# Attention and product-key experts on one core: heads summed in two groups by TensorE, attention's sums inverted on ScalarE, and new orders on every engine

## The reference, cut to what matters

```
q   = xn @ wq.T                       # 2 halves, 8 heads, 64 wide
sim = q . keys                        # per half and head 32 scores
sx, ix = top_k(sim[0], 16);  sy, iy = top_k(sim[1], 16)
scores, pk = top_k(sx[:, None] + sy[None, :], 16)     # of 256 pairs
h   = gelu(xn . table_down[indices]) * softmax(scores)
out = sum over 8 heads and 16 picks of h * table_up[indices]
```

## Time and profile before

| | us |
|---|---|
| median of 3 runs | 1073.86 (1070.39 to 1075.57) |
| the profiled execution, own time | 1074.99 |
| its span, first to last instruction | 1073.2 |
| VectorE busy | 931.1 |
| TensorE busy (matmuls) | 764.6 |
| ScalarE busy | 704.9 |
| GpSimd busy | 656.5 |
| mean granted clock of TensorE | 0.89 |

### The profile page before, as it was taken

One profiled execution on the slowest core, in us unless ns is written; L12 is line 12 of the kernel. 1 busy time (PEld: TensorE's weight loads), 2 busy tenths in 40 slices (PEclk: granted clock), 3 DMA queues, 4 the chain that ended last, 5 costly groups with the idle time before them and its releaser, 6 DMA issues.

```text
span 1073.2 us, 22148 instructions
## 1 busy us (share of the span) xinstructions
PE 764.6 (71%) x6014; PEld 474.0 (44%) x6014; DVE 931.1 (87%) x4054; ACT 704.9 (66%) x1008; POOL 656.5 (61%) x371
## 2 busy tenths in 40 slices
PE   3672868686777878586777768686767878776374
PEld 2431525354444535354444535354444545353253
DVE  3327289999999999899999989899999989998987
ACT  1352677676867676676867676676867676756461
POOL 2101077694948576694948576694948576674942
PEclk9695979898998989898999989898998989797766
DMA  5312103030212103030212102030212102000000
GB/s 145 51 21 34 17 13 38 1 52 1 39 15 37 16 13 40 0 53 1 38 15 38 16 14 40 0 53 1 39 15 38 16 13 37 1 11 2 5 1 10
DMA packets 51538, 26.51 MB, mean 25 GB/s; under 512 B 5168, under 2 KB 51120, under 8 KB 51312
## 3 DMA queue, kind: packets, MB, share of 16 engines
q1 hardware_dynamic: 51504, 26.11, 15.0%
HBM read 19.93 MB, written 5.24 MB: 23 GB/s over the span
## 4 chain that ended last, share of the span: by engine, by line
DVE 38%; PE 34%; ACT 12%; issue 11%; DMA 1%; SPq 1%; POOL 1%; DVEq 1%; ACTq 0%; POOLq 0%
DVE prob L910 13%; DVE late_scores L777 6%; PE misc L1131 5%; ACT prob L640 4%; PE score L1192 4%; PE score L1081 4%; PE score L1111 3%; PE score L1161 3%; PE score L1204 2%; DVE cand L856 2%; PE misc L1133 2%; DVE cand_left L874 2%; ACT late_scores L544 2%; PE misc L1220 2%; DVE halves L771 2%
## 5 line engine op out<-in xcount | busy, mean ns | idle before, releaser
L449 POOL TENSOR_TENSOR acc<-acc,prob 128x1024 f32<-128x1024 f32 x186 | 441.7, 2375 | 16.6 <-DVE prob L910 0.5
L910 DVE SCALAR_TENSOR_TENSOR prob<-score,cut,prob 128x1024 f32<-128x1024 f32 x256 | 316.7, 1277 | 37.4 <-ACT prob L640 36.0
L640 ACT ACTIVATE prob<-score,neg_lse,unit 128x1024 f32<-128x1024 f32 x256 | 299.4, 1201 | 65.4 <-PE score L1192 51.3
L1192 PE MATMUL score<-sel,pieces_t 128*128 128x512 f16 x512 | 177.3, 447 | 102.3 <-DVE prob L910 97.5
L561 ACT ACTIVATE probs<-score 128x512 f32<-128x512 f32 x192 | 107.6, 599 | 64.7 <-PE score L1113 63.2
L422 POOL TENSOR_TENSOR scale<-bounded,half_neg 128x2 f32<-128x2 f32 x16 | 11.2, 703 | 202.7 <-DVE bounded L821 202.7
L1192 PEld LDWEIGHTS score<-sel,pieces_t 128*128 128x128 f16 x512 | 43.3, 108 | 183.6 <-DVE prob L910 151.6
L544 ACT ACTIVATE late_scores<-score 128x512 bf16<-128x512 f32 x128 | 69.6, 594 | 67.3 <-PE score L1084 62.2
L1111 PE MATMUL score<-q_stack,k_stack 128*128 128x512 bf16 x192 | 76.1, 401 | 45.9 <-DVE prob L910 23.5
L1081 PE MATMUL score<-k_ahead,q_ahead 128*128 128x256 bf16 (+1 forms) x512 | 75.9, 253 | 44.3 <-ACT probs L561 18.8
L449 POOL TENSOR_TENSOR acc<-prob 128x1024 f32<-128x1024 f32 x31 | 73.2, 2361 | 44.2 <-DVE prob L910 44.2
(11 more groups left out here) (119 smaller groups left out, 1549.4 us busy)
## 6 DMA issues: line engine op xcount, KB each, us to landing
q_ahead<-q_scratch SPq DMA_DIRECT2D x96, 64.0 KB
q_stack<-q_scratch SPq DMA_DIRECT2D x96, 64.0 KB
q_scratch<-qk_piece SPq DMA_DIRECT2D x16, 192.0 KB, 2.4
xin<-x SPq DMA_DIRECT2D x16, 128.0 KB, 4.7
xres<-x SPq DMA_DIRECT2D x16, 128.0 KB, 5.1
out<-fin SPq DMA_DIRECT2D x16, 128.0 KB, 5.6
k_ahead<-qk_piece SPq DMA_DIRECT2D x96, 4.0 KB
k_stack<-qk_piece SPq DMA_DIRECT2D x96, 4.0 KB
```

The source lines that it names most:

```text
L449: eng.tensor_tensor(acc[:, j, :], so_far, prob[:, j * FH + h, :], ALU.add).then_inc(acc_added, 1)
L640: eng.activation(prob[:, g, :], score[g % BUFS][:, :], ACT.Exp, bias=neg_lse[:, j, h:h + 1], scale=unit[:, :]).then_inc(prob_made, 1)
L910: eng.scalar_tensor_tensor(prob[:, g, :], score[g % BUFS][:, :], cut[:, j, h:h + 1], prob[:, g, :], ALU.is_ge, ALU.mult).then_inc(prob_mas ...
L1192: ins = eng.matmul(score[g % BUFS][:, cols], pieces_t[:, j, h, :], sel[:, cols], start=True, stop=True)
```

## The change

The heads of a tile are no longer added into one tensor. GpSimd adds heads 1, 2, 3 onto head 0 and 5, 6, 7 onto head 4, in place in `prob` (six additions a tile, `ADDS` = 6), and `acc` is gone. TensorE makes the transposed sum: for each of the eight blocks it multiplies the group's block with the identity twice, and PSUM accumulates. Head 0 and head 4 of a tile may be overwritten a batch later only when TensorE has read them (`acc_tp`). VectorE's additions of the last tile go the same way.

The inverse of attention's sums is Ln and then Exp with scale -1 on ScalarE (`invert_sums`), not a reciprocal on VectorE. `select_pairs` is split into `sum_pairs` (the five additions and the size) and the selection.

The orders change on four engines: on GpSimd make_xhat comes ahead of make_xn; on ScalarE the inversion stands behind the copies of x2 and ahead of all twelve score copies, `best_exp` of tile 0 among these, `activate` behind `log_sum`; on VectorE ln1 and make_y come directly behind the second key selection, ahead of the candidates, and the folding ahead of the second tile's candidates; on TensorE the value matmuls come directly behind attention's scores, then the scores for the maxima with project_y and the second tile's sums among them. The diff, cut to its core:

```diff
+GROUP = 4
+ADDS = FH - FH // GROUP
+def added(j, h):
+    return j * ADDS + h - h // GROUP
...
             def add_head(b, j, h):
                 eng.wait_ge(prob_masked, at(prob_masked, b, j * FH + h + 1))
-                ...
-                eng.tensor_tensor(acc[:, j, :], so_far, prob[:, j * FH + h, :], ALU.add).then_inc(acc_added, 1)
+                if h % GROUP > 1:
+                    eng.wait_ge(acc_added, at(acc_added, b, added(j, h - 1)))
+                group = prob[:, j * FH + h - h % GROUP, :]
+                eng.tensor_tensor(group, group, prob[:, j * FH + h, :], ALU.add).then_inc(acc_added, 1)
...
             def iteration(i, d, f, a, m, p):
-                if a:
-                    make_xn(i + 1)
                 if p:
                     make_xhat(i + 3)
                 if a:
+                    make_xn(i + 1)
                     sim_low_piece(i + 1, 0)
...
+            def invert_sums(b):
+                eng.wait_ge(av_made, every(av_made, b))
+                if later(b):
+                    eng.wait_ge(proj_made, at(proj_made, b, 0))
+                eng.activation(y_t[:, :], misc[0][:, T:2 * T], ACT.Ln).then_inc(y_log, 1)
+                eng.wait_ge(y_log, every(y_log, b))
+                eng.activation(y_t[:, :], y_t[:, :], ACT.Exp, scale=-1.0).then_inc(y_inverse, 1)
...
             def pair_probs(b, j, h):
-                    eng.wait_ge(acc_added, at(acc_added, b - 1, j * (FH - 1) + max(h, 1)))
+                    if h % GROUP:
+                        eng.wait_ge(acc_added, at(acc_added, b - 1, added(j, h)))
+                    else:
+                        eng.wait_ge(acc_tp, at(acc_tp, b - 1, j + 1))
...
                 if f:
                     pieces_back(i, 1)
-                if m:
-                    for u in range(6):
-                        max_scores_back(i + 2, u)
                 if d and f:
                     age_x2(i - 1)
                 if f:
                     copy_x2(i)
+                if a:
+                    invert_sums(i + 1)
                 if m:
-                    for u in range(6, MAX_STEPS):
+                    copy_v(i + 2)
+                    for u in range(9):
                         max_scores_back(i + 2, u)
-                    copy_v(i + 2)
                 if f:
+                    best_exp(i, 0)
+                if m:
+                    for u in range(9, MAX_STEPS):
+                        max_scores_back(i + 2, u)
+                if f:
+                    log_sum(i, 0)
                     activate(i, 0)
                     activate(i, 1)
...
             def make_y(b):
-                if later(b):
-                    eng.wait_ge(proj_made, at(proj_made, b, 0))
                 eng.wait_ge(av_made, every(av_made, b))
-                eng.reciprocal(y_t[:, :], misc[0][:, T:2 * T]).then_inc(y_inverse, 1)
                 eng.wait_ge(y_inverse, every(y_inverse, b))
...
                 if f:
                     select_keys(i, 1)
+                if p:
+                    ln1(i + 3)
+                if a:
+                    make_y(i + 1)
+                if f:
+                    sum_pairs(i, 0)
                     select_pairs(i, 0)
                 if a:
-                    make_y(i + 1)
+                    make_x2(i + 1)
                 if d:
                     gate(i - 1, 1)
-                if a:
-                    make_x2(i + 1)
-                if f:
-                    select_pairs(i, 1)
+                if f:
                     sum_best(i, 0)
-                if p:
-                    ln1(i + 3)
-                if f:
-                    log_sum_exp(i, 0)
                 if m:
                     fold_max(i + 2, 0, 6)
                 if f:
+                    sum_pairs(i, 1)
+                    log_sum_exp(i, 0)
+                    select_pairs(i, 1)
+                if f:
+                    mask(i, 0, 0)
+                    mask(i, 0, 1)
                     sum_best(i, 1)
-                    for h in range(4):
-                        mask(i, 0, h)
+                    mask(i, 0, 2)
+                    mask(i, 0, 3)
                     log_sum_exp(i, 1)
...
                 for c in range(CH):
-                    ins = eng.transpose(score[j][:, c * P:(c + 1) * P], acc[:, j, c * P:(c + 1) * P], ident[:, :])
+                    for h in range(0, FH, GROUP):
+                        ins = eng.matmul(score[j][:, c * P:(c + 1) * P], prob[:, j * FH + h, c * P:(c + 1) * P],
+                                         ident[:, :], start=h == 0, stop=h == FH - GROUP)
...
-                if m:
-                    for u in range(6):
-                        scores_for_max(i + 2, u)
                 if a:
                     weigh_values(i + 1, 0, piece_t_made, i)
                     weigh_values(i + 1, 1, piece_t_made, i)
                 if m:
-                    for u in range(6, MAX_STEPS):
+                    for u in range(4):
+                        scores_for_max(i + 2, u)
+                if a:
+                    project_y(i + 1, piece_t_made, i)
+                if m:
+                    for u in range(4, 8):
                         scores_for_max(i + 2, u)
                 if d:
                     acc_transposes(i - 1, 1)
+                if m:
+                    for u in range(8, MAX_STEPS):
+                        scores_for_max(i + 2, u)
                 if f:
                     hidden_units(i, 0)
-                if a:
-                    project_y(i + 1, piece_t_made, i)
-                if f:
                     hidden_units(i, 1)
                 if a:
                     xn_transpose(i + 1, y_t_made, i + 1)
                 if f:
-                    pair_scores(i, 0, 0, a, m)
+                    for h in range(3):
+                        pair_scores(i, 0, h, a, m)
...
                 if p:
                     project_qkv(i + 3, sim_kept, i + 1)
                 if f:
-                    for h in range(5, FH):
-                        pair_scores(i, 0, h, a, m)
+                    pair_scores(i, 0, 5, a, m)
+                    pair_scores(i, 0, 6, a, m)
+                if p:
+                    eng.wait_ge(v_next_made, every(v_next_made, i + 3))
+                    keep_busy(misc[0], 2)
+                if f:
+                    pair_scores(i, 0, 7, a, m)
+                if p:
+                    keep_busy(misc[0], 2)
```

More of the change, by code:

```diff
@@ L208, in build @@
         av_made = signal("av_made")
+        y_log = signal("y_log")
         y_inverse = signal("y_inverse")
@@ L241, in build @@
         prob_masked = signal("prob_masked", TILES * FH)
-        acc_added = signal("acc_added", TILES * (FH - 1))
-        late_added = signal("late_added", FH - 1)
+        acc_added = signal("acc_added", TILES * ADDS)
+        late_added = signal("late_added", ADDS)
         x2_copied = signal("x2_copied")
@@ L480, in iteration @@
                 if f:
-                    add_head(i, 0, 1)
-                    add_head(i, 0, 2)
-                    add_head(i, 0, 3)
+                    for h in range(1, GROUP):
+                        add_head(i, 0, h)
                 if p:
@@ L486, in iteration @@
                 if f:
-                    for h in range(4, FH):
+                    for h in range(GROUP + 1, FH):
                         add_head(i, 0, h)
@@ L659, in prologue @@
                 xhat_back(2)
+                invert_sums(0)
                 for u in range(MAX_STEPS):
@@ L690, in iteration @@
                     copy_x2(i)
+                if a:
+                    invert_sums(i + 1)
                 if m:
-                    for u in range(6, MAX_STEPS):
+                    copy_v(i + 2)
+                    for u in range(9):
                         max_scores_back(i + 2, u)
-                    copy_v(i + 2)
                 if f:
+                    best_exp(i, 0)
[4 more added lines that the diff above has]
+                    log_sum(i, 0)
                     activate(i, 0)
                     activate(i, 1)
-                    best_exp(i, 0)
                 if a:
@@ L701, in iteration @@
                 if f:
-                    best_exp(i, 1)
-                    log_sum(i, 0)
                     pair_probs(i, 0, 0)
+                    pair_probs(i, 0, 1)
                 if a:
@@ L708, in iteration @@
                 if f:
-                    pair_probs(i, 0, 1)
+                    best_exp(i, 1)
+                if f:
+                    pair_probs(i, 0, 2)
                 if a:
@@ L713, in iteration @@
                 if f:
-                    pair_probs(i, 0, 2)
+                    log_sum(i, 1)
+                    pair_probs(i, 0, 3)
                 if p:
@@ L861, in select_pairs @@
                                   apply_absolute_value=True).then_inc(pair_step, 1)
-                n += len(PAIR_BLOCKS)
+            def select_pairs(b, j):
+                n = j * PAIR_STEPS + len(PAIR_BLOCKS)
```

(15 more changed lines are left out.)

21 lines of the change are left out of this document (5 added, 16 removed).

## The result

The changed kernel takes 1110.83 us (median of 4 runs, 1108.33 to 1113.41), the kernel before 1073.88 beside it: a ratio of 1.0349, 95% interval 1.0308 to 1.0389. That is 37 us more. It is slower, by the mechanism that was forecast, and 9 us more than the forecast.

What follows compares the result with a forecast made beforehand. No engine was full, so order inside an iteration and waits between engines were taken to decide. Twelve iterations by 2.2 us (+26.4) and the ends gave +28: 1102 us against the median, range 1050 to 1120.

Steps and rivals of the forecast that it cites:

- The waits: VectorE's waits in one iteration of the new order, at gates, product of y, folding and masks: together 10.9 us.
- all 6.4 us of VectorE's work: VectorE loses per iteration the reciprocal (1.75), the candidates' collision with GpSimd (3.2) and the folding's (1.5).
- two places: VectorE's candidate additions and its folding, where the new order would end collisions with GpSimd costing 3.2 and 1.5 us.
- 62.7: Length in us of the walked iteration after the change, 2.2 more than 60.54.
- +26.4 of the sum: Iterations 1 to 12 together: 12 by 2.2 us, the largest term of the total +28.
- The second rival: Clock falls while TensorE idles 2.2 before the value matmuls, which take 5.4 more: 1165 us, chance 0.04.
- The first rival: Clock stays up in the qkv projection, which takes 1.2 us: period 61.5, time 1088 us, chance 0.20.
- Iteration 13: The iteration behind the twelve, without a projection: 2.7 us more.
- One instruction a matmul: TensorE's sums at the transposes' 0.11 a matmul, both 1.75 us: period 59.0, time 1051 us, chance 0.05.
- VectorE's work counts more than the waits: Added waits lie inside each other, 7 us left of 10.9: period 58.4, time 1045 us, chance 0.13.
- No change: Time not told from the kernel before: clock up and one us less of waits, chance 0.10.
- Four times: Skill's fp32 price against transpose mode: a sum of 7.0 us, 3.4 more each on 28 sums: 1195 us, chance 0.02.

Runs made afterwards that it cites:

- e2: e1 with eight ordinary fp32 matmuls with the identity for a tile's sum instead of eight transposes; 1065.26 us, ratio 0.9915.
- e3: The kernel before with only two groups of four and TensorE's 16 matmuls, old orders and reciprocal kept; 1138.22 us, ratio 1.0603.
- e11: The changed kernel with unused matmuls ahead of the qkv projection, behind the last head and ahead of the value matmuls; 1083.13 us, ratio 1.0078.
- e9: e8 with 14 more unused matmuls ahead of the value matmuls; 1021.79 us, ratio 0.9518.
- e1: The changed kernel with one group of eight: GpSimd adds all heads, TensorE sums by eight transposes; 1046.59 us, ratio 0.9733.
- e6: e1 with the first tile's five candidate additions moved ahead of the product of y; 1044.43 us, ratio 0.9731.
- e5: e1 with 15 unused matmuls a period ahead of heads 3 and 4 and the qkv projection; 1044.89 us, ratio 0.9731.
- e8: e1 with the changes of e5 and e6, and 12 unused matmuls instead of 4 behind tile 1's last head; 1029.08 us, ratio 0.9582.

## Why the prediction was right, and where its terms were off

**The steps that held.** The waits were the right ones, in the right places. Predicted and measured, in order: first gate 0.75 and 0.56; product of y 4.15 and 4.30; second gate 1.4 and 1.09; folding 1.4 and 1.39; mask 4, 0.2 and 0.24; mask 5, 2.3 and 1.40; behind it 0.7 and 0.60. Together 10.9 and 9.58. The sums end at T + 5.99 (6.0 walked), the seventh exponential starts at 6.52 (6.53), the value matmuls at 11.81 (11.83), the product at 18.21 (18.2). The candidates take 0.87 for either tile, the folding 4.4 up to what follows it (444.20 to 448.57), the reciprocal is gone: all 6.4 us of VectorE's work went. e2 settles the price of a matmul, and e3 that the sums alone are the loss.

**A collision not seen.** The walk had 51.4 us of VectorE's work in a period; 62.14 less 9.58 is 52.56. The 1.2 us are the row at 458.64: tile 1's neg_lse takes 1.45, where tile 0's takes 0.21 (at 449.48) and tile 1's in the walked iteration of the kernel before took 0.22. GpSimd's first addition had begun at 457.71:

```profile
457.71 7.22 POOL L452 TENSOR_TENSOR prob<-prob 128x1024 f32<-128x1024 f32 x3
```

A third of 7.22 is 2.41; the first addition ends at 460.1, and so does neg_lse (460.09). The prediction took the collision away at two places and did not ask where the shifted additions meet VectorE next. Here it costs little, since mask 5 waits for the projection in any case, and the 1.2 come out of that wait.

**Why 62.14 and not 62.7.** The second sum starts at T + 22.18 (22.9 walked), the folding at 28.87 (29.6) and the projection at 42.40 (43.25); mask 5 stands 4.95 behind the projection and not 4.7, and the rest takes 14.8 as walked. The kernel before missed the other way: its walked iteration has 60.54 us, the mean of the twelve 60.30.

**The clock.** The forecast had the projection at half clock and all else at full, in every period. In five of twelve it was also low elsewhere and the period 1.6 to 1.7 longer. Without that the 12 iterations would have given +22.0; with it they gave +30.3. So the +26.4 of the sum came nearer than its parts: the short period was walked too long, the dips were left out, and the two misses cancel in part. That is luck. The second rival (the clock falls before the value matmuls, 5.4 a period, 0.04) was right on the place in three of the twelve periods, and too high by three times on the size, since only about half of those matmuls run slowly. In two periods the dip was at the start, which the prediction does not name. The first rival (the clock stays up in the projection) did not come about, but e11 makes its case: 1083 where it said 1088.

**The ends.** Iteration 13 cost +6.9, not +2.7. It began at half clock (gate wait 2.31, wait for y 5.14), and its masks waited for head scores that ran at half clock from 962 to 971, the fourth window above. This is the mis-sized term that weighs most, 4.2 us. In e11, where that iteration starts at full clock, it takes 60.77 and not 63.55, so 2.8 of them are clock. Iteration 0 kept 1.3 of gain, not 2.5. The tail's 64 instructions took 10.1 until the next (9.5 walked); iteration 15 with it +1.7, not +0.5. The sum of the terms was 28, the measured one 38.3, and the forecast on the median 9 us low.

**The rivals that fell.** One instruction a matmul: 1024 instructions, and 1.78 us for 8. VectorE's work counts more than the waits: it asked that the waits lie inside each other, 7 us of them left; 9.58 are. No change: not in this kernel, nearly in e11. Four times: 2.05.

Small slips in the working changed nothing: the selection among the candidates is put at 3.75, where the row named gives 3.85, and two rivals stand at 1165 and 1195, where 12 times 5.4 and 28 times 3.4 give 1167 and 1197.

**What wins instead.** The change had a gain of 29 us and a loss of 64 in it. e9 keeps the first, drops the second, moves one step and holds the clock up: 4.8% faster than the kernel before and 8% than the changed one.

## What to carry to other kernels

Price work that is moved to another engine by who is queued behind it there, not by that engine's idle share: TensorE was 71% busy or less, and yet 2.7 us twice a period cost 64 us. Judge the parts of a change separately; a gain may be real and sit under another part's wait (the inversion: nothing here, 11 us in e1). Where a wait is removed, look for the next wait and the next dip of the clock before calling the edit useless, and compare periods of the same kind: two edits that could not be told from nothing in the median won 17.5 us together with a third. And look into every kind of period, not into one: the five longer ones here lose their time in two places.

## What the runs showed of the hardware

- Two kinds of VectorE's operations with two or more inputs in SBUF were held up to the end of the GpSimd addition beside them, the candidate additions (4.09 us in place of 0.88, and 3.08 in e6) and neg_lse, small as it is: 128x8 took 1.45 us in place of 0.21. The Trainium skill, "GPSIMD Engine Reference", Specifications, names the shared SBUF interfaces for operations with two SBUF inputs; this trace agrees. A hold has the length of what is left of one addition, 2.42 us at most here; of the five candidate additions of the kernel before, two were held, 1.32 and 2.42 us long, by two additions of GpSimd.
- It goes the other way too. GpSimd's xhat beside VectorE's folding in the kernel before:

```profile
437.82 1.06 POOL L397 TENSOR_TENSOR xhat<-xin,mv 128x256 f32<-128x256 f32 x1
439.02 1.41 POOL L401 TENSOR_TENSOR xhat<-xhat,rstd 128x256 f32<-128x256 f32 x1
```

  and in the changed kernel, where VectorE waits for y meanwhile, 0.61 each:

```profile
429.99 0.61 POOL L404 TENSOR_TENSOR xhat<-xin,mv 128x256 f32<-128x256 f32 x1
430.75 0.61 POOL L408 TENSOR_TENSOR xhat<-xhat,rstd 128x256 f32<-128x256 f32 x1
```

- Filling one sparse stretch of TensorE won the clock there and left it to fall elsewhere. In the profiled executions, of 12 periods each: e1 has the projection low in all, the value matmuls in three and the start in two; e5, which fills ahead of the projection, the value matmuls in six and a stretch near T + 36 in three; e8 the same; e9 only that stretch, in five; both of these also T + 18 in the first period; e11, whose TensorE is also busy with the sums, none. What decides the place stays open.
